# Routed experts: rows scattered into fixed rooms and loaded plainly, results accumulated by the scatter

## The reference

```python
logits = x @ gate_w.T                      # 1024 tokens, 16 experts in 4 groups
scores = sigmoid(logits); sb = scores + gate_bias
# a group's score is the sum of its two best; the best 2 groups stay; 4 best experts of these
w = scores[chosen] / (sum(scores[chosen]) + 1e-20) * 2.5
y = sum over the 4 chosen e of  w_e * (silu(x @ w1[e].T) * (x @ w3[e].T)) @ w2[e].T
y = y + (silu(x @ ws1.T) * (x @ ws3.T)) @ ws2.T      # the shared expert
x = x + tanh(g_ffn[1]) * y
```

## Time and profile before

| | us |
|---|---|
| median of 3 runs (1140.32 to 1142.3) | 1140.37 |
| profiled execution, its device time | 1141.2 |
| profiled execution, its span | 1139.4 |
| PE busy | 995.2 (87%) |
| DVE busy | 827.9 (73%) |
| ACT busy | 710.7 (62%) |
| POOL busy | 424.0 (37%) |

### The profile page before, as it was taken

How to read it: one execution, slowest core, us unless ns; L and a number is a source line. 1 busy time by engine, 2 the same in 40 slices (tenths; PEclk the granted TensorE clock), 3 DMA queues, 4 the chain that set the end, 5 groups by cost and what they waited for, 6 DMA issues and landing times. The chain is left out here.

```text
span 1139.4 us, 18929 instructions
## 1 busy us (share of the span) xinstructions
PE 995.2 (87%) x6572; PEld 875.3 (77%) x6572; DVE 827.9 (73%) x1594; ACT 710.7 (62%) x1377; POOL 424.0 (37%) x442
## 2 busy tenths in 40 slices
PE   1789979898899989999999999999999978588981
PEld 1668878688688768898888889898888867487870
DVE  6687765777623379788888888788888966774645
ACT  3477756776633468777777777777787833074550
POOL 5164432543167700402003020402006463767771
PEclk9899989999999999999999999999999999699996
DMA  4100000000311200000100001000001323253335
GB/s 132 33 1 1 1 5 1 1 1 14 103 42 35 68 1 1 1 1 2 38 1 1 1 1 38 1 1 1 14 16 41 95 70 88 60 168 101 104 103 203
DMA packets 41437, 45.38 MB, mean 40 GB/s; under 512 B 15040, under 2 KB 35648, under 8 KB 40832
## 3 DMA queue, kind: packets, MB, share of 16 engines
q1 hardware_dynamic: 36832, 31.84, 9.2%
q0 software_dynamic: 4512, 12.33, 3.6%
HBM read 35.89 MB, written 8.26 MB: 39 GB/s over the span
## 5 line engine op out<-in xcount | busy, mean ns | idle before, releaser
L331 PE MATMUL PS<-R 128*128 128x512 f32 (+3 forms) x2669 | 574.8, 359 | 40.2 <-POOL R L539 7.9
L331 PEld LDWEIGHTS PS<-R 128*128 128x128 f32 x2669 | 427.9, 194 | 98.7 <-issue 22.5
L1641 DVE TENSOR_TENSOR R<-PS,R 128x512 fp32r<-128x512 f32 x320 | 205.1, 682 | 37.6 <-ACT R L1314 36.6
L1314 ACT ACTIVATE R<-PS 128x512 fp32r<-128x512 f32 x320 | 174.6, 596 | 79.1 <-PE PS L773 78.0
L1277 ACT ACTIVATE FA<-PS,nmax 128x1024 f32<-128x1024 f32 (+1 forms) x160 | 192.6, 1204 | 35.6 <-DVE nmax L1630 18.9
L786 PE MATMUL PS<-R 128*128 128x256 f32 x1408 | 202.6, 289 | 10.5 <-DVE FB L1649 9.1
L773 PE MATMUL PS<-eye,FA 128*128 128x128 f32 x1408 | 185.3, 276 | 13.4 <-DVE R L1641 5.2
L773 PEld LDWEIGHTS PS<-eye,FA 128*128 128x128 f32 x1408 | 160.8, 141 | 46.0 <-issue 21.3
L786 PEld LDWEIGHTS PS<-R 128*128 128x128 f32 x1408 | 178.8, 190 | 18.7 <-issue 14.5
L1630 DVE TENSOR_REDUCE nmax<-PS 128x1 f32<-128x1024 f32 x128 | 155.5, 1220 | 33.9 <-PE PS L331 23.4
L497 POOL TENSOR_SCALAR R<-R 64x512 fp32r<-64x512 f32 x40 | 25.8, 645 | 320.2 <-ACT R L1429 260.0
(11 more groups left out here) (234 smaller groups left out, 1241.6 us busy)
## 6 DMA issues: line engine op xcount, KB each, us to landing
wst<-w_in SPq DMA_DIRECT2D x4, 1024.0 KB, 4.9
wst<-we_in SPq DMA_DIRECT2D x16, 256.0 KB
wst<-we_in SPq DMA_DIRECT2D x24, 128.0 KB
FB<-k_in SPq DMA_DIRECT2D x16, 128.0 KB, 2.0
FA<-parts SPq DMA_DIRECT2D x4, 512.0 KB, 4.9
wst<-w_in SPq DMA_DIRECT2D x3, 512.0 KB, 7.2
x<-x_in SPq DMA_DIRECT2D x2, 512.0 KB, 6.2
FB<-ctxT_in SPq DMA_DIRECT2D x2, 512.0 KB, 4.4
```

The lines of the kernel that those rows point to most:

```text
L331: last = mm(out, a, b, start=(n == 0), stop=(n == len(passes) - 1), skip_group_check=skip)
L1314: a_(L.pt[0][:, (u // 2) % 2, 4 * g_:4 * g_ + 4, (u % 2) * P:(u % 2) * P + P], L.turn(u, g_).rearrange("p (t n) -> p t n", t=4), ACT.Copy) ...
L1641: inc(v.tensor_tensor(lo, turned, hi.bitcast(F32), ALU.subtract), "p_lo")
```

## The change

Before the tiles:

- HBM tensor `rows_d` gets a fixed room of 1024 rows for each of 16 experts plus 128 rows. A row is 273 words (`ROW`): 256 of the token, 16 of its chosen scores by expert, and its token number. Three sums (`sums_d`, each 1024 + 128 rows of 256) replace `parts_d`.
- Early in layer 1's attention SP fills all rows with zeros and a spare row number, and the sums with zeros, by six transfers from a small tile `fill`.
- Routing works on batch 0 and batch 1 apart (`CHUNKS`). Batch 0's rows are turned, split and sent through the router inside the last attention block (u = 9 to 13), its sigmoid is taken at u = 15, and DVE's `choose(0)` runs at u = 16. `find_slots(c)` turns ranks into row numbers of the rooms.
- POOL scatters each token's row to its four rooms (`place_rows`): 16 indirect DMAs for each batch. The table, its one-hots and its matmuls go.
- POOL keeps the subtractions of `expert_lo` for experts 3 to 10; ACT makes the high parts.

In the tiles: SP loads tile j with one plain transfer from `rows_d`, at a row number read into a register, into one of eight buffers `got`. DVE's `tile_share` picks each row's score for the tile's expert and ACT's `rows_out` multiplies by it. POOL's only transfer per tile is an indirect DMA that adds the 128 rows into sum j mod 3; it waits until the last transfer into that sum, tile j-3's, has landed. A buffer of `got` is loaded again after tile j-8's scatter has landed.

After the tiles: SP loads the three sums in twelve transfers of 256 KB; DVE adds them, scales by the token's inverse sum and adds into `x`.

The diff, cut:

```diff
+ROOM = NB * S
+ROW = D + E + 1
+HELD = 8
+PLANES = 3
+CHUNKS = ((0, 4), (4, 4))
+SPLIT_POOL = 11
+HI_AT = {1: 9, 2: 10, 4: 11, 6: 12, 8: 13, 10: 14, 12: 15}
+LO_AT = {5: 11, 7: 12, 9: 13, 11: 14, 13: 15}
+LOAD_AT = {3: (9, 10), 7: (11, 12), 9: (13,), 11: (14,), 13: (15,)}
...
@@ SP @@
+        sp.wait_ge(s["preset"], 1)
+        every = rows_d.rearrange("(c p) n -> p c n", p=P)
+        for c in range(0, E * ROOM // P + 1, 43):
+            sp.dma_start(every[:, c:c + 43, :], fill.unsqueeze(1).to_broadcast([P, 43, ROW])).then_inc(s["filled"], 16)
+        for i in range(PLANES):
+            sp.dma_start(sums_d[i]..., fill[:, 0:D]...).then_inc(s["filled"], 16)
...
+        for c, (t0, n) in enumerate(CHUNKS):
+            sp.wait_ge(s[f"placed_rows{c}"], 64 * n)
+        sp.wait_ge(s["places_set"], 1)
+        for j in range(TILES):
+            if j % 4 == 0:
+                sp.reg_load(regs[0:n], places[0:1, j:j + n])
+            if j >= HELD:
+                sp.wait_ge(s[f"sent{j % PLANES}"], 16 * ((j - HELD) // PLANES + 1))
+            sp.dma_start(got[:, j % HELD, :], rows_d[bass.ds(at[j % 4], P), :]).then_inc(s[f"got{j % HELD}"], 16)
+            for e in LOAD_AT.get(j, ()):
+                next_expert(e)
+        for w in range(4):
+            for i in range(PLANES):
+                sp.dma_start(back[i][w]..., sums_d[i][2 * w * P:2 * w * P + 2 * P, :]...)
@@ POOL @@
-        for e in range(9):
-            expert_split(e)
+        for e in range(3):
             expert_split(e)
+        pool.wait_ge(s["at_lo"], 4 + 4 * NG1)
+        for h in range(2):          # before16: iota and tensor_scalar, each waited for
...
+        expert_lo(3); expert_lo(4)          # two subtractions each
+        place_rows(0)
+        expert_lo(5); expert_lo(6)
+        place_rows(1)
+        for e in range(7, SPLIT_POOL):
+            expert_lo(e)
+        for j in range(TILES):
+            plane = j % PLANES
             pool.wait_ge(s["y_out"], j + 1)
+            if j >= PLANES:
+                pool.wait_ge(s[f"sent{plane}"], 16 * (j // PLANES))
+            g.indirect_dma_start(sums_d[plane], <row number in got>, put[:, j % RINGS, :], None,
+                                 compute_op=ALU.add).then_inc(s[f"sent{plane}"], 16)
+        def place_rows(c):
+            for t in range(t0, t0 + n):
+                for k in range(4):
+                    g.indirect_dma_start(rows_d, <slots[:, 4 * t + k]>, row_tiles[t], None)
@@ PE, last block @@
+                if not more and u in (9, 11):      # 4 transposes of late0 each
+                if not more and u == 13:
+                    router(0)
...
+                pe.wait_ge(s["gate_sig"], 1)
                 out_rows(L1, C)
+                rank(0)
                 out_project(L1, b, C)
@@ ACT @@
+                elif u == 15:
+                    route_scores(0)                # sigmoid of batch 0
+            a_(put[:, j % RINGS, :], PS[:, 6 + j % 2, 0:256], ACT.Copy, scale=tile_weight[:, j:j + 1])
@@ DVE @@
+                elif u == 16:
+                    choose(0)                      # 41 instructions, before out_sum(7) at u = 18
             if not more:
-                split_norm(3 * NB + 1, 0)
                 out_norm(L1, C)
                 out_lo(L1, b, C)
+                find_slots(0)
...
         split_norm(3 * NB + 2, 1)
+        choose(1)
         job(1, 1)
+        find_slots(1)
         job_low(1, 1)
...
+        def tile_share(j):
+            inc(v.tensor_tensor_reduce(share, share, owned[:, j, :], 1.0, 0.0, ALU.mult, ALU.add,
+                                       accum_out=tile_weight[:, j:j + 1]), "weight_set")
...
+        for w in range(4):
+            dve.wait_ge(s[f"back_in{w}"], 16 * PLANES)
+            for i in range(1, PLANES):
+                do(v.tensor_tensor(back[0][w], back[0][w], back[i][w], ALU.add))       # 128 x 512
+            for t in (2 * w, 2 * w + 1):
+                inc(v.scalar_tensor_tensor(x[:, t, :], ..., inverse[:, t:t + 1], x[:, t, :], ALU.mult, ALU.add), "out_ready")
```

More of the change, by code:

```diff
@@ L260, in program @@
+    offsets, places = (FB[0:1, 1792 + 48 * i:1840 + 48 * i].bitcast(I32) for i in range(2))
     earlier, all_ones = R[:, 9920:10048], R[:, 10048:10176]
     taken = R[:, 9472:9616]
[L262 to L270, removed]
-    raw_in, raw_out = [wst[:, 768 * r:768 * r + 768] for r in range(2)], [xs[:, 0:512], wst[:, 1536:2048]]
-    rows_d = nc.dram_tensor("rows", (NB * S, D), F32, kind="Internal").ap()
-    parts_d = nc.dram_tensor("parts", (SPARE_ROWS + P * 48, D), F32, kind="Internal").ap()
-    got = FB[:, 0:1024].rearrange("p (r n) -> p r n", r=RINGS)
+    fill = xs[:, 0:ROW]
@@ L611, in _ @@
                 pair1_low(2, 3)
+        pool.wait_ge(s["ln_turned"], 2 * NB)
+        step(g.memset(fill, 0.0))
+        step.wait()
+        g.iota(fill[:, ROW - 1:ROW].bitcast(I32), [[0, 1]], base=NB * S, channel_multiplier=1).then_inc(s["preset"], 1)
+        pool.wait_ge(s["preset"], 1)
         copy_queries(L1, 2, (5, 6))
@@ L700, in scatter @@
-        def scatter(j):
-            r = j % RINGS
-            pool.wait_ge(s["y_out"], j + 1)
[L703 to L728, removed]
+        pool.wait_ge(s["rbc"], 2 * (2 * NG1 + 2))
@@ new lines, in _ @@
+        expert_lo(4)
+        def place_rows(c):
+            t0, n = CHUNKS[c]
+            pool.wait_ge(s["slots_set"], c + 1)
+            for t in range(t0, t0 + n):
+                for k in range(4):
+                    i = 4 * t + k
+                    g.indirect_dma_start(rows_d, bass.IndirectOffsetOnAxis(ap=slots[:, i:i + 1], axis=0), row_tiles[t],
+                                         None).then_inc(s[f"placed_rows{c}"], 16)
+        pool.wait_ge(s["filled"], 16 * (3 + PLANES))
@@ L1040, in router, with rank @@
                                 for kt in range(KT)])
-                last = group(PS[:, 3, t * E:t * E + E], passes)
+                last = group(PS[:, 3 if b else 5, t * E:t * E + E], passes)
             last.then_inc(s["gate_done"], 1)
+        def rank(c):
+            t0, n = CHUNKS[c]
+            first, width = E * t0, E * n if c == 0 else 144 - E * t0
+            out = PS[:, 0 if c else 3, 256:256 + width]
+            if c:
+                pe.wait_ge(s["e_full"], 1)
+            pe.wait_ge(s["consts"], 1)
+            pe.wait_ge(s["taken_set"], c + 1)
+            mm(out, earlier, taken[:, first:first + width], start=True, stop=False, skip_group_check=True)
+            for t in range(t0 + n - (c == 0)):
+                skip = max(0, t + 1 - t0)
+                left = width // E - skip
+                last = mm(out[:, E * skip:].rearrange("p (t e) -> p t e", e=E), all_ones,
+                          taken[:, E * t:E * t + E].unsqueeze(1).to_broadcast([P, left, E]),
+                          start=False, stop=(t == t0 + n - 1 - (c == 0)), skip_group_check=True)
+            last.then_inc(s["ranked"], 1)
         def block(C, b, wo=None, wq=None, late=True, more=True):
@@ L1160, in _ @@
             zero_banks(7)
+        rank(1)
         down(1, 0, 1)
+        pe.wait_ge(s["slots_set"], 2)
+        gate_up(2, 1, 0)
         gate_up(3, 1, 1)
         down(2, 1, 0)
[L1165 to L1173, removed]
-        down(3, 1, 1)
[L1175 to L1178, removed]
-                last = mm(PS[:, 1, 48 * k:48 * k + 48], same_slot[:, 4 * t + k, :], same_tile[:, 4 * t + k, :],
-                          start=(t == 0 and k == 0), stop=(t == NT - 1 and k == 3), skip_group_check=True)
-        last.then_inc(s["tabled"], 1)
+        down(3, 1, 1)
         regs = [pe.alloc_register(f"weights{i}") for i in range(8)]
@@ L1500, in _ @@
         ln_split(3 * NB + 2, 1, LNH)
[L1501 to L1516 removed]
+        route_scores(1)
+        expert_hi(5)
+        job(1, 1)
+        expert_hi(6)
+        job(2, 0)
+        job(3, 1)
+        expert_hi(7)
+        expert_hi(8)
         def rows_hi(j):
@@ L1535, in rows_out @@
             if j >= RINGS:
-                act.wait_ge(s[f"sent{j % RINGS}"], 16 * (j // RINGS))
-            a_(put[:, j % RINGS, :], PS[:, 6 + j % 2, 0:256], ACT.Copy).then_inc(s["y_out"], 1)
-        expert_hi(10)
+                act.wait_ge(s[f"sent{j % PLANES}"], 16 * ((j - RINGS) // PLANES + 1))
+            act.wait_ge(s["weight_set"], j + 1)
+            a_(put[:, j % RINGS, :], PS[:, 6 + j % 2, 0:256], ACT.Copy, scale=tile_weight[:, j:j + 1]).then_inc(s["y_out"], 1)
         rows_hi(0)
@@ new lines, in find_slots @@
+        def find_slots(c):
+            t0, n = CHUNKS[c]
+            place, slot = bo[:, 0:E * n].rearrange("p (t e) -> p t e", e=E), bo[:, 64:64 + 4 * n]
+            ranks = PS[:, 0 if c else 3, 256:256 + E * n].rearrange("p (t e) -> p t e", e=E)
+            dve.wait_ge(s["ranked"], c + 1)
+            do(v.tensor_tensor(place, ranks, room_at.unsqueeze(1).to_broadcast([P, n, E]), ALU.add))
+            for t in range(n):
+                last = v.tensor_tensor(product[:, 4 * t:4 * t + 4, :], chosen[:, t],
```

(12 more changed lines are left out.)

418 lines of the change are left out of this document (209 added, 209 removed).

## The result

The changed kernel takes 1215.37 us in the median (1215.19 to 1215.91), the kernel before, run beside it, 1141.34: a ratio of 1.0644, interval 1.063 to 1.0659. The prediction, 1129.8 with a range up to 1150, was wrong. The profiled execution spans 1214.1 where the sum said 1128.8. Those 85.3 us lie almost wholly in one term. The first `tile_gate_up` starts at 1001.78 (997.2 forecast, 4.6 of the miss); from it to the last scatter at 1193.98 it is 192.2 instead of 112.1 (80.1); landing and combination take 20.1 instead of 19.5 (0.6).

What follows compares the result with a forecast made beforehand. POOL's two indirect transfers, 2.57 per tile, were taken to bound the tiles. Lost 9.6 ahead, won 15.6 in tiles, lost 0.8 in landing, won 5.4 behind: span 1128.8, median 1129.8, range 1121 to 1150.

Steps and rivals of the forecast that it cites:

- Accumulating: Adding scatters in the tiles: landing taken as 3.2, hidden up to 4.85 by eight buffers, costing only 0.8 at the end.
- Tiles: Tile loop: PE becomes the bound at 2.15 per tile over 46 tiles, plus 8 for the start; last scatter at 1109.3.
- the start, charged at 8: First tiles: slower than PE's steady pace through low clock and weight waits, 8 us, bounds 3 and 13.
- End of attention: Last attention block: batch 0's routing on DVE loses its cover, `at_lo` at 935.0 instead of 927.06, 7.9 lost.
- POOL up to the first tile: From `at_lo` to the tiles: POOL's splits and 32 scatters put the first `tile_gate_up` at 997.2, 9.6 lost.
- meetings with DVE: Before the tiles: placing scatters held up by DVE on the shared SBUF port, charged 1.0, up to 20 if all were.
- Filling: HBM fill during attention: 21.6 MB, 97 us from about 395, done before the weight load at 564.2; charged nothing.
- Landing and combination: After the tiles: last landing 3.2, then loading and adding the sums and storing, 16.1 instead of 21.5.
- The first: Rival in the tiles: adding lands later than 4.85, each tile costs a third of the excess; 1158 at 7.0; chance 0.20.
- its limit: In the tiles: the landing time of an adding transfer that eight buffers were said to hide, 4.85.
- The second: Rival in the tiles: adding costs POOL twice the issue, 2.57 per tile, 19 more, 1149; chance 0.08.

Runs made afterwards that it cites:

- right wait: Changed kernel with one index put right, so load j waits for the sum tile j-8 was added to: 1146.17 against 1144.11 before, ratio 1.0023.
- the transfers overwriting: Kernel with the right wait, but POOL's result transfers overwrite the sums instead of adding, losing parts: 1138.17 against 1143.83 before, ratio 0.9954.
- the splits moved: Kernel with the right wait, low-part splits of experts 5 to 7 moved from POOL to DVE, later splits and loads rearranged: 1141.65 against 1143.83 before.
- the loads later: Kernel with the splits moved, weight loads of experts 12 to 14 one tile later in SP's list: 1140.5 against 1142.43 before, ratio 0.9985.

## Why the prediction was wrong

**The step that failed** is the one on the buffers under "Accumulating": "The eight buffers are tighter: `turn_rows(j+8)` comes three iterations and 1.3 behind". Its frame was right, its depth was not: the wait as written holds every third load for tile j-6. With tile j-6 the slack is one iteration: 2.15 + 1.3 - 2.9 = 0.55, by the same working, against a landing of 3.8. Some 3.25 per three tiles then shows, in 13 threes 42 us. Measured it is about twice that: from 1027.76 to 1181.42 three tiles take 12.8 on average, 6.35 over three of the forecast's 2.15, and 13 times that is 83, near the 80.1 of the miss. One loop as measured: scatter at 1057.31, rows turned at 1064.59 (landing, load and waking, 7.3, where the working gives 6.1 with a landing of 3.8), the scatter three tiles on at 1070.73 (PE's way to it, 6.1 at the low clock, where the working gives 3.7). The right wait gives 69 us back, and six buffers alone take them all again.

**Tiles.** With the right wait POOL's transfers are 2.08 apart in steady runs, but 2.27 on average, 0.12 over the forecast. From the first gate matmul to the last scatter it is then 124.9, 12.8 over the forecast's 112.1. With the transfers overwriting it is 118.1, so some 6.8 of the 12.8 is adding, by these two executions; "up to there it costs only its last landing, 0.8" was too little even with the right wait. The rest lies in the start, charged at 8. There POOL splits 9 and 10 ahead of its first accumulating scatter (1015.06), and PE waits 3.9 for rows twice; but with the splits moved this scatter comes at 1000.62, and 1000.18 with the loads later, and the way from the first gate matmul to the last scatter is still 128.5 and 124.0. So what the start costs beyond 8 stays open.

**End of attention.** `at_lo` comes at 937.2, forecast 935.0; in the kernel with the right wait at 934.7. `choose(0)` takes 6.3 in one piece, 7.3 forecast.

**POOL up to the first tile.** The 32 scatters take 42.1 in two pieces, 41.0 and the 1.0 for meetings with DVE forecast. What I missed is the other direction: DVE waits for POOL's subtractions, 4.3 in `owned`. The Trainium skill (SBUF — State Buffer, "Who interferes with whom") has the rule for both; I weighed it for the scatters alone. By that rule two SBUF inputs make DVE wait while POOL reads SBUF; the trace agrees, 5.25 in `owned` beside POOL's subtractions and 0.96 without them. The 4.3 were worth about 1.1 on the way to the first gate matmul. That this matmul came at 1001.78 and not at 997.2 is not this term's doing: in the three kernels with the same code up to there it comes at 996.3 to 996.5, and what the changed kernel is behind them arises mostly ahead of routing (see Filling).

**Landing and combination.** The last landing took 3.7 instead of 3.2, and from landing to the end 16.4 instead of 16.1.

**Filling.** The changed kernel is 3.3 behind the one before ahead of the fill and 3.7 behind after it, so the fill costs at most 0.4, as charged. The 3.3 arise in code that the change does not touch; kernels here with the same code up to there start the fill between 394.8 and 398.7.

**Rivals.** The first had the right picture, PE waiting behind SP's wait, with the wrong cause: the landing stayed under its limit. The second is half true: 1.55 instead of 0.97 to issue, which fits into PE's 2.08. Of the chances, 0.27 stood on slower, none on this: no rival doubted how deep the ring is.

## What to carry to other kernels

Where the wait of a ring is written with another modulus than the ring's own, work out for each residue which earlier item it really waits for, before pricing anything: one index was worth 69 us. Price a ring as a loop (landing, reload, the consumer's way back) and compare it with the depth; below that, each cost that was hidden shows in full. A list that mixes loads with different conditions is as late as its strictest wait, so place a load where its buffer is already free, not as early as possible.

## What the runs showed of the hardware

An indirect transfer of 128 rows of 1 KB that adds in HBM takes POOL 1.55 to issue against 0.96 for one that overwrites, and lands in 3.8 to 4.0 against 2.4 in the six-deep loop and 3.1 in the eight-deep one. While POOL ran four subtractions back to back, a DVE conversion of 128 x 16 stood for 6.06 and ended with the last of them (kernel with the right wait, 0.17 where it met none); it was not let in between two of them:

```profile
963.57 6.06 DVE L2034 CAST FB<-bo 128x16 uint32<-128x16 f32 x1
```

In the same kernel `tile_share`, a small operation of 128 x 16, stood for 0.47 and 1.13 instead of 0.17 beside four other subtractions, each time only to the end of the one under way. That DVE is always held to the end of the four is therefore not shown.

PE's 11 matmuls behind a wait of 4.4 to 4.6 took 3.33 at a granted clock of 0.50 (1051.3 to 1055 in the changed kernel, the lower of the two levels, 1.2 GHz), and 1.89 once it ran without pauses at 1.00: a starved ring pays a second time, in the clock. What the low clock alone cost is not shown: with six buffers and shorter waits the clock was 0.91 and the time the same, but there every tile waits and not every third.
